# Second attention: two heads share 32 result rows, and two of four value products move into the next round

## The reference

```
q = (x @ wq).reshape(B, T, 16, 8)
lat = x @ w_down
k, v = lat @ wk_up, lat @ wv_up          # per head 8 wide
q, k = rope(q), rope(k)
scores = einsum('bqhd,bkhd->bhqk', q, k) / sqrt(8)
scores = where(page(k) <= page(q), scores, lowest)   # pages of 32 tokens
out = einsum('bhqk,bkhd->bqhd', softmax(scores), v).reshape(B, T, 128)
x = x + out @ wo
```

## Time and profile before

| what | value |
|---|---|
| median of 3 runs | 492.01 us (491.33 to 493.22) |
| the profiled execution | 490.57 us, span 488.7 us |
| mean granted TensorE clock | 0.92 of full speed |
| TensorE busy | 84% of the span, 411.0 us |
| DVE, ACT, POOL busy | 63%, 47%, 44% |

### The profile page before, as it was taken

The page is one execution under the profiler, slowest core; times in us unless marked ns, Lnnn a source line. Parts: engine busy times, 40 slices in busy tenths (PEclk is TensorE's granted clock), DMA queues, the critical chain, the costliest instruction groups (busy, mean ns, idle before and its releaser), DMA issues.

```text
span 488.7 us, 15624 instructions
## 1 busy us (share of the span) xinstructions
PE 411.0 (84%) x5250; PEld 320.9 (66%) x5251; DVE 309.4 (63%) x1125; ACT 231.5 (47%) x565; POOL 214.2 (44%) x312
## 2 busy tenths in 40 slices
PE   8898899998657899977679989989888888698980
PEld 7777588885547899854446555655555567598880
DVE  4776588888564555369557568568877655454543
ACT  2687556766304555211226756756655420255540
POOL 5443345555641444325643635643822434133440
PEclk9999999999769999988858999999999876799995
DMA  8999900000001121120000000000000000112116
GB/s 237 297 217 347 275 15 9 7 11 12 24 16 45 56 65 54 40 85 1 2 1 2 1 1 3 1 0 0 1 2 7 30 23 22 35 50 64 55 48 182
DMA packets 44339, 28.60 MB, mean 59 GB/s; under 512 B 7200, under 2 KB 40480, under 8 KB 44288
## 3 DMA queue, kind: packets, MB, share of 16 engines
q1 hardware_dynamic: 38096, 20.83, 15.4%
q0 software_dynamic: 2496, 5.13, 2.9%
q10 hardware_dynamic: 3696, 1.97, 1.4%
HBM read 12.76 MB, written 15.16 MB: 57 GB/s over the span
## 4 chain that ended last, share of the span: by engine, by line
PE 58%; DVE 17%; issue 8%; DMA 7%; ACT 5%; DVEq 2%; POOL 2%; SPq 0%; POOLq 0%; ACTq 0%
PE S L1435 7%; PE bank L1445 6%; PE S L1343 6%; PE bank L1302 6%; PE bank L1319 3%; PE bank L1475 3%; PE bank L1558 3%; DVE nm L756 3%; DMA slots<-yo,token 2%; PE bank L1329 2%; PE bank L1248 2%; PE bank L1569 2%; PE bank L1254 2%; PE S L1275 2%; DMA xg<-rows 2%
## 5 line engine op out<-in xcount | busy, mean ns | idle before, releaser
L915 ACT ACTIVATE E<-S,nmax 128x256 f32<-128x256 f32 x128 | 59.0, 477 | 39.2 <-DVE nmax L541 39.2
L1148 POOL DMA_INDIRECT slots<-yo,token x46 | 44.1, 958 | 75.5 <-DVE yo L697 74.1
L1011 ACT ACTIVATE E<-S 128x1536 f32<-128x1536 f32 x32 | 46.4, 1450 | 24.4 <-PE S L1534 24.3
L1107 POOL TENSOR_TENSOR vs<-Va,rden 128x512 f32<-128x512 f32 x32 | 33.3, 1040 | 50.5 <-DVE rden L576 48.6
L1435 PE MATMUL S<-xgT,W1s 128*128 128x128 f32 x368 | 52.9, 289 | 1.4 <-DVE xgT L683 1.3
L972 ACT ACTIVATE hT<-S,b 128x128 f32<-128x128 f32 x92 | 28.7, 363 | 44.2 <-PE S L1435 44.2
L1445 PE MATMUL bank<-W,hT 128*128 x368 | 49.2, 277 | 0.2
L1435 PEld LDWEIGHTS S<-xgT,W1s 128*128 128x128 f32 x368 | 46.2, 197 | 4.5 <-issue 2.2
L756 DVE TENSOR_REDUCE nm<-bank 128x2 f32<-128x512 f32 x64 | 41.0, 683 | 9.1 <-PE bank L1501 9.1
L1445 PEld LDWEIGHTS bank<-W,hT 128*128 128x128 f32 x368 | 45.2, 194 | 0.5 <-issue 0.5
L541 DVE TENSOR_REDUCE nmax<-S 128x4 f32<-128x1024 f32 x32 | 39.0, 1218 | 7.2 <-PE S L1343 6.8
(11 more groups left out here) (181 smaller groups left out, 954.9 us busy)
## 6 DMA issues: line engine op xcount, KB each, us to landing
rows<-zeros SPq DMA_DIRECT2D x1, 8768.0 KB, 31.5
xg<-rows SPq DMA_DIRECT2D x46, 64.5 KB
W<-in_L_ffn_W SPq DMA_DIRECT2D x1, 2048.0 KB, 10.2
x<-in_L_attn_a_x SPq DMA_DIRECT2D x4, 256.0 KB, 5.4
yg<-slots SPq DMA_DIRECT2D x8, 128.0 KB, 3.5
yg<-slots ACTq DMA_DIRECT2D x8, 128.0 KB, 3.9
slots<-yo,token POOLq DMA_INDIRECT x46
yg<-in_select SPq DMA_DIRECT2D x1, 512.0 KB, 7.8
```

The lines of the kernel that those rows point to most:

```text
L915: last = act.activation(E[:, hp, h, c, :], S[hp % 2][:, h, c * T:(c + 1) * T], ACT.Exp, bias=nmax[:, hp, k:k + 1], accum_out=den[:, hp, k: ...
L1011: act.activation(Eb[:, q % 2, :, :], S4[:, 0:3, :], ACT.Exp, scale=SCALE_B).then_inc(bs["exp"], 1)
L1107: pool.tensor_tensor(vs[:, q, :, :, :], v, r, ALU.mult).then_inc(a_vs, 1)
L1148: pool.indirect_dma_start(out=y_dram, out_offset=bass.IndirectOffsetOnAxis(token[:, turn_at, :], 0), in_=yo[:, turn_at % 2, :], in_offset=None
```

## The change

Two heads share the 32 columns: in `Vb` the heads of an even block have their values in columns 0 to 7 and a one in 8, those of an odd block in columns 16 to 23 and a one in 24. Blocks 0 and 1 (and 2 and 3) are now added into the same rows of `pb[1]`, so that a batch has two blocks of results. ACT copies two blocks out and not four; four transposes and not eight turn them back; one division does all of `att`. As the heads now lie in another order, `wo` is loaded by rows, head by head. The value products of blocks 2 and 3 both run at the start of the next round, and the fourth scores move ahead of the transposes L1623.

```diff
@@ SyncE
-            sp.dma_start(wo[:, :], wo_in).then_inc(b_loaded, 16)
...
+            for g in range(HB):
+                h = head_at(g)
+                sp.dma_start(wo[g * DB:(g + 1) * DB, :], wo_in[h * DB:(h + 1) * DB, :]).then_inc(wo_loaded, 16)
@@ the order of heads
+        def head_at(g):
+            return 8 * (g // 8) + 4 * (g % 2) + (g % 8) // 2
+        def heads(t, q):
+            return t.rearrange("p (k q j) r -> p k q j r", q=2, j=4)[:, :, q, :, :]
@@ DVE
-            def b_normal(b, u):
-                dve.wait_ge(bs["on"], b * 2 + u + 1)
-                o = pb[1][:, :].rearrange("p (h r) -> p h r", r=32)
-                dve.reciprocal(rsum[:, u, :], o[:, :, DB]).then_inc(bs["rsum"], 1)
...
+            def b_normal(b):
+                dve.wait_ge(bs["on"], b + 1)
+                o = pb[1][:, :].rearrange("p (g r) -> p g r", r=16)
+                r = rsum[:, :, :].rearrange("p u h -> p (u h)")
+                dve.reciprocal(r, o[:, :, DB]).then_inc(bs["rsum"], 1)
+                dve.wait_ge(bs["rsum"], b + 1)
                 waits(dve, bs["at"], b)
+                dve.tensor_tensor(att.rearrange("p u (h d) -> p (u h) d", d=DB), o[:, :, 0:DB],
+                                  r.unsqueeze(2).to_broadcast([P, 2 * HB, DB]), ALU.mult
...
-                if l: b_normal(b - 1, 0)
+                if l: b_normal(b - 1)
...
-                if l: b_normal(b - 1, 1)
@@ ACT
-            def b_outT(b, p, q):
-                act.wait_ge(bs["pv"], b * 4 + q + 1)
-                act.copy(OTb[:, p, q, :], pb[1][:, 0:T]).then_inc(bs["ot"], 1)
+            def b_outT(b, p, k):
+                act.wait_ge(bs["pv"], b * 4 + 2 * k + 2)
+                act.copy(OTb[:, p, k, :], pb[1][:, 0:T]).then_inc(bs["ot"], 1)
...
-                if l: b_outT(b - 1, 1 - p, 3)
+                if l: b_outT(b - 1, 1 - p, 1)
...
-                if c: b_outT(b, p, 0)
...
-                if c: b_outT(b, p, 1)
+                if c: b_outT(b, p, 0)
...
-                if c: b_outT(b, p, 2)
@@ POOL
-                z = zeros[:, :].rearrange("p (h d) -> p h d", d=DB)
-                for u in range(2):
-                    last = pool.tensor_tensor(Vb[:, p, u, :, 0:DB], vst[:, p, u, :].rearrange("p (h d) -> p h d", d=DB), z,
-                                              ALU.add)
+                z = zeros[:, :].rearrange("p (k j d) -> p k j d", j=4, d=DB)
+                for q in range(2):
+                    last = pool.tensor_tensor(heads(Vb[:, p, :, :, :].rearrange("p u h r -> p (u h) r"), q)[:, :, :, 16 * q:16 * q + DB],
+                                              heads(vst[:, p, :, :].rearrange("p u (h d) -> p (u h) d", d=DB), q), z, ALU.add)
@@ TensorE, b_values: L1558, then L1561
-                              Eb[:, q % 2, h % 2, (h // 2) * T:(h // 2 + 1) * T], start=True, stop=False)
+                              Eb[:, q % 2, h % 2, (h // 2) * T:(h // 2 + 1) * T], start=(q % 2 == 0), stop=False)
...
-                                     Eb[:, q % 2, 2, h * P:(h + 1) * P], start=False, stop=True)
+                                     Eb[:, q % 2, 2, h * P:(h + 1) * P], start=False, stop=(q % 2 == 1))
@@ TensorE, b_natural
-                for q in range(4):
-                    last = pe.transpose(pb[1][:, q * P:(q + 1) * P], OTb[:, p, q, u * P:(u + 1) * P], ident)
+                for u in range(2):
+                    for k in range(2):
+                        last = pe.transpose(pb[1][:, (2 * u + k) * P:(2 * u + k + 1) * P],
+                                            OTb[:, p, k, u * P:(u + 1) * P], ident)
@@ TensorE, b_round
                 if l:
                     waits(pe, bs["x"], b - 1)
+                    pe.wait_ge(bs["ot"], b * 2 - 1)
+                    b_values(b - 1, 1 - p, 2)
                     b_values(b - 1, 1 - p, 3)
...
-                if l: b_natural(b - 1, 1 - p, 0)
+                if l: b_natural(b - 1, 1 - p)
...
                 if c:
-                    waits(pe, bs["att"], b * 2 - 1)
+                    waits(pe, bs["att"], b)
                     b_values(b, p, 0)
                 if n: b_tk(b + 1, 1 - p, 1)
-                if l:
-                    if c: pe.wait_ge(bs["ot"], b * 4 + 1)
-                    else: pe.wait_ge(bs["att"], b * 2 - 1)
-                    b_natural(b - 1, 1 - p, 1)
...
                     b_values(b, p, 1)
+                if n: b_scores(b + 1, 1 - p, 3)
                 if l:
-                    pe.wait_ge(bs["att"], b * 2)
-                    if c: pe.wait_ge(bs["ot"], b * 4 + 2)
+                    pe.wait_ge(bs["att"], b)
+                    if c: pe.wait_ge(bs["ot"], b * 2 + 1)
                     for u in range(2):
                         last = pe.transpose(pb[1][:, u * P:(u + 1) * P], att[:, u, :], ident)
...
-                if n: b_scores(b + 1, 1 - p, 3)
                 if nnn: b_kv(b + 3)
-                if l and c: pe.wait_ge(bs["attT"], b)
-                if c:
-                    pe.wait_ge(bs["ot"], b * 4 + 2)
-                    b_values(b, p, 2)
-                    b_scoresT(b, p, 3)
-                    pe.wait_ge(bs["ot"], b * 4 + 3)
+                if c: b_scoresT(b, p, 3)
...
                 if l:
-                    if not c: pe.wait_ge(bs["attT"], b)
+                    pe.wait_ge(bs["attT"], b)
```

More of the change, by code:

```diff
@@ L181, in build @@
         OTb = vs[:, :, :, :, :].rearrange("p s h c n -> p (s h c n)").rearrange(
-            "p (a q t) -> p a q t", a=2, t=T)
+            "p (a q t) -> p a q t", a=2, t=T)[:, :, 0:2, :]
         spare = OT[:, :, :, :, :].rearrange("p h j s i -> p (h j s i)").rearrange("p (k u c) -> p k u c", k=2, u=2)
@@ L232, in build @@
         b_loaded = sem("b_loaded")
+        wo_loaded = sem("wo_loaded")
         sel_loaded = sem("sel_loaded")
@@ L1092, in _ @@
             pool.wait_ge(bs["const"], 2)
-            pool.memset(Vb[:, :, :, :, DB:DB + 1], 1.0).then_inc(bs["const"], 1)
+            for q in range(2):
+                pool.memset(heads(Vb[:, :, :, :, :].rearrange("p a u h r -> p (a u h) r"), q)[:, :, :, 16 * q + DB:16 * q + DB + 1],
+                            1.0).then_inc(bs["const"], 1)
             def a_stage(b, p):
@@ L1558, in b_values, with b_natural @@
                     pe.matmul(pb[1][32 * h:32 * h + 32, 0:T], Vb[:, p, 0, 4 * q + h, :],
-                              Eb[:, q % 2, h % 2, (h // 2) * T:(h // 2 + 1) * T], start=True, stop=False)
+                              Eb[:, q % 2, h % 2, (h // 2) * T:(h // 2 + 1) * T], start=(q % 2 == 0), stop=False)
                 for h in range(4):
                     last = pe.matmul(pb[1][32 * h:32 * h + 32, P:T], Vb[:, p, 1, 4 * q + h, :],
-                                     Eb[:, q % 2, 2, h * P:(h + 1) * P], start=False, stop=True)
+                                     Eb[:, q % 2, 2, h * P:(h + 1) * P], start=False, stop=(q % 2 == 1))
                 last.then_inc(bs["pv"], 1)
-            def b_natural(b, p, u):
-                if u == 0:
-                    pe.wait_ge(bs["ot"], b * 4 + 4)
-                for q in range(4):
-                    last = pe.transpose(pb[1][:, q * P:(q + 1) * P], OTb[:, p, q, u * P:(u + 1) * P], ident)
+            def b_natural(b, p):
+                pe.wait_ge(bs["ot"], b * 2 + 2)
+                for u in range(2):
+                    for k in range(2):
+                        last = pe.transpose(pb[1][:, (2 * u + k) * P:(2 * u + k + 1) * P],
+                                            OTb[:, p, k, u * P:(u + 1) * P], ident)
                 last.then_inc(bs["on"], 1)
@@ L1615, in b_round @@
                 if c:
-                    if l: pe.wait_ge(bs["att"], b * 2)
-                    else: pe.wait_ge(bs["ot"], b * 4 + 1)
                     b_values(b, p, 1)
+                if n: b_scores(b + 1, 1 - p, 3)
                 if l:
-                    pe.wait_ge(bs["att"], b * 2)
-                    if c: pe.wait_ge(bs["ot"], b * 4 + 2)
+                    pe.wait_ge(bs["att"], b)
+                    if c: pe.wait_ge(bs["ot"], b * 2 + 1)
                     for u in range(2):
@@ L1675, in b_router @@
                     what(router_at(b, point))
-            pe.wait_ge(b_loaded, 80)
-            pe.wait_ge(bs["const"], 3)
+            pe.wait_ge(b_loaded, 64)
+            pe.wait_ge(wo_loaded, 16 * HB)
+            pe.wait_ge(bs["const"], 4)
             pe.wait_ge(copied, len(copies))
```

3 lines of the change are left out of this document (removed).

## The result

The kernel after the change takes 500.1 us (median of four runs, 498.6 to 504.24) against 491.92 for the kernel before on the same chip (491.33 to 493.22): a ratio of 1.0151, with a 95% interval of 1.010 to 1.020. It is slower by some 8 us. I had forecast 492.4 with 495.2 as the upper end.

The account below looks back on a forecast made before the run. A fixed 6.8 us of DVE and POOL was taken to bound each round's end, not TensorE. Terms +1.5 + 0.9 - 1.3 + 0.8 - 1.4 = +0.5 us gave a median of 492.4, range 488.9 to 495.2.

Parts of the forecast that it names:

- The end of the round: TensorE ready for mask transposes 0.9 us before POOL, worth nothing; rounds 5 and 6 +0.8 us together.
- rival 3: Clock falls at the end of rounds 5 and 6: one fall costs 2.5 us, 495; two, 497; chance 0.22.
- The closing rounds: Rounds 7 and 8, with extra and leaving blocks and the second return removed: total -1.4 us, bounds -3.4 and 0.
- Deferred block: Round start, two value blocks where one stood: +0.4 us in round 3, +0.79 in round 6, +1.5 over six.
- One division for two: DVE's larger division ahead of the first maxima makes TensorE wait: +0.15 us a round, +0.9 over six.
- Second return gone: Second four return transposes go, but third scores wait for ACT's key copy: 0.22 us gained a round, -1.3 over six.
- The later L1634: End of rounds 5 and 6, attention transposes behind the fourth scores: +0.54 us in round 6, about half in round 5.
- TensorE's busy time: Sign of being right: TensorE busy 0.5 us less in each of rounds 1 to 4.
- The loads: Sixteen loads of wo for one, 586 ns each on SP's queue, behind the zero fill: priced at 0.
- The signs I had named: Right: rounds 1 to 4 at 17.1 to 17.6 us; wrong: near 16.5, or clock below 1 between 355 and 375.
- Rival 1: TensorE is the bound after all, in rounds and closing rounds: 483.6 us, or 488 for half; chance together 0.14.
- Rival 2: Closing rounds keep the upper clock: -2 us on top, 488.9 us with two stretches; chance 0.12.

Follow-up runs that it names:

- e3: Kernel after with two unread products ahead of each pair of mask transposes; 497.31 us, ratio 1.0066.
- e2: Kernel after with the one old load of wo, rows in the old order of heads; 501.42 us, ratio 1.012.
- e4: Kernel after with mask transposes and ACT's mask copy moved into the next round, behind query transposes and first value block; 493.16 us, ratio 0.999.
- e1: Kernel before with sixteen loads of wo for one; 493.45 us, ratio 0.997.
- e6: Kernel before with two unread products in round -1; five of six runs between 495.1 and 499.6 us, one 487.2, no ratio.
- e7: Kernel before with only the fourth scores moved ahead of the attention transposes L1623; 494.44 us, ratio 1.003.
- e9: Kernel before with two unread products in round 7 alone; 490.5 us, ratio 0.986.
- e5: e4 plus two unread products in round -1 and in round 7; 488.37 us, ratio 0.994 against the kernel before.
- e10: e5 with round 6's router products moved ahead of the value blocks; 490.08 us, ratio 0.985 against the kernel before.
- e11: Kernel before with mask transposes moved behind the next query transposes and the unread products of e5; 488.56 us, ratio 0.990.
- e8: Kernel after with round 6's router products moved ahead of the two value blocks; 498.41 us, ratio 1.012 against the kernel before.

## Why the prediction was wrong

**The step that failed** is "The end of the round": TensorE is ready 0.9 us before POOL, and "This is worth nothing". For the position of the mask transposes this was exact: in round 3 they follow the third scores by 7.23 us for 7.24, and the idle time in front of them is 0.7 us in rounds 2 to 4. But a wait that hides behind POOL isn't free when the clock answers to it. The 1.00 us at 272.98 and the 2.02 us at 381.82 were followed by the lower level, and e3, which fills them and moves nothing else, gives back 1.32 and 2.69 us. I had this as rival 3, with "some 2 us in one piece" (2.02 measured) and a chance of 0.22, and didn't put it into the likeliest sum because one wait of 1.26 us had stayed without a fall. Two things were off in it. I looked at rounds 5 and 6 alone and not at round 0, whose end gets the same shape. And I priced a fall at 2.5 us; they cost 1.3 and 2.7, so the size was fair on average and the number of places was not: my range ended at one fall.

**The closing rounds**, -1.4, are the second step that failed. With the clock as much at the lower level as before (0.78 in before and 0.77 in e3 from the last mask transposes to the totals, 17 to 18 us of it at 0.50), e3 needs 38.60 us and before 38.36: +0.24. Split at the router's third and fourth logits (L1254; L1267 in e3), the first value products of round 8 and the last attention transposes (L1623; L1634), it is:

```
stretch, from the end of the one above     before    e3    difference   clock before, e3
last mask transposes to third logits        10.43  10.94     +0.51        1.00  0.99
to fourth logits                             7.43   6.45     -0.98        0.54  0.50
to the value products of round 8             2.79   4.19     +1.40        1.00  0.57
to the attention transposes                  4.09   3.63     -0.46        0.98  1.00
to the totals                               13.62  13.39     -0.23        0.63  0.72
```

```profile
393.59:396.38 2.79, 2.74 (x19) 2.27 (x18) 1.86 (x12) 1.71 (x2) 0.55 (x1) 1.00 0.08 25
400.17:404.36 4.19, 4.19 (x20) 3.87 (x19) 2.46 (x15) 1.82 (x2) 1.80 (x3) 0.57 0.12 35
```

The first row is of before, the second of e3. Most edges are near their terms: +0.51 where I had 0.55 for the third router step, -0.46 where round 8 was to give 0.79 less 1.21. The block that leaves gave -0.98 where 1.44 and 0.1 of wait were to go, with a lower clock here too. What takes the rest back is where the lower level lies. In before it is over when the output product and the products behind it come; in e3 it lasts on through them, and the stretch needs 1.40 us more. The same holds in after, e2 and e4, whose stretch at 0.50 that begins near the third logits lasts 10.2 us, against 6.8 in before, e1 and e6. Whether the wait of 1.25 us in front of e3's third logits (0.20 in before) makes it longer is not tested. e7's -1.1 does not show that the early fourth scores gain by themselves: it has 3.5 us less at 0.50, which is worth more than that by the price below.

**The edges** came out near their terms, but for round 5, which cost twice its term. In us, the sum of my terms for rounds 1 to 6 against the measured differences (for round 1 that of e3, whose clock stays up there):

```
round        1      2      3      4      5      6     sum
terms      -0.04  -0.07  +0.33  -0.02  +0.41  +1.26  +1.9
measured   +0.05  +0.08  +0.48  +0.04  +0.84  +1.29  +2.8
```

- *Deferred block.* From the mask transposes to the key transposes round 3 needs 2.67 us for 2.39 (311.86 - 309.19; 308.14 - 305.75), +0.28 where I had +0.4. In round 6 the first scores come at 369.70 and 364.01, that is +0.89 after their mask transposes; I had +0.79 and the division.
- *One division for two.* L787 0.42 us as forecast, L784 0.36 for 0.26: +0.23 a round and not +0.15. That is 0.5 us of the 0.9 by which the table's sums differ.
- *Second return gone.* The third scores are released by ACT's key copy, as forecast (0.29 us of idle time, 319.82).
- *The later L1634* in rounds 5 and 6: e7 measures it alone, 0.29 and 0.55 for 0.28 and 0.54.
- *TensorE's busy time* was to fall by 0.5 us in rounds 1 to 4; it fell by 0.03 to 0.06 in rounds 2 and 4. Groups that contain a wait count as busy (the third scores take 0.53 us for four where the unhindered ones take 0.39), so the measure did not suit. What makes up the rest I did not follow.
- *The loads*, priced at 0: e1 and e2 bear it out.

In sum: rounds +2.8, closing +0.2, clock +4.0, makes 7.0 us, which is what the trace shows from the first mask transposes on. The medians differ by 8.2. The remaining 1.2 us are within what single executions differ by ahead of the second attention (2.05 us between the two profiled ones, 5.3 between before and e9, whose code there is the same); I can't say more about them. Against my sum of +0.5 the 7.7 us that are missing are 4.0 of clock, 0.9 of edges, 1.6 of closing rounds and these 1.2.

**The signs I had named.** Those of being right came for the lengths of rounds 2 and 4, the release of the third scores, the division and round 6, and the wait in front of the mask transposes with 0.7 us for 0.8 to 1; they failed for rounds 1 and 3 and for the closing rounds. Neither sign of being wrong came: the clock stood at 1.00 from 355 to 375 and fell outside the stretch that I had named.

**The other rivals.** Rival 1 (TensorE is the bound): rounds 2 and 4 did not shorten, and e7's filled waits moved nothing, so no. Rival 2 (closing rounds keep the upper clock): the opposite came, though the upper level is worth what it supposed: e9, with 1.1 us of unread products, holds it to about 402 us, 21 us behind its last mask transposes where before held it for 11, and closes in 1.4 us less.

## What to carry to other kernels

Ahead of a wait that another engine ends, work taken off TensorE shortened nothing here and lengthened what followed, as the clock fell behind the longer wait: look at the granted clock of the stretch behind every wait that a change makes longer, in every round that has it and not in the one that was studied, and in more than one trace. What helped was to have TensorE do something there, by moving the waiting instruction behind work that is ready (e4, e5) or by a few products that nobody reads (e3, e9); neither kept the clock up each time (e5 near 275 us, e10 from 380). And before a change is credited with a gain, the same repair belongs on the kernel without it: e11 showed that the change had brought nothing of e5's gain in the rounds at full clock.

## What the hardware showed that I had not expected

- Waits of 1.00 us were followed by the lower level in after and e2 (e2: 1.00 us in front of 274.38, granted 0.53 from 274 to 276). In e8 1.01 us at the same place (272.75) were not, and its round 1 lasts 17.54 us. At the end of round 5, 2.02 us of wait left the clock at 1.00 in after and e2 and were followed by 0.50 in e8. At the end of round 6 the same 2.02 us were followed by a fall in all three. Before, e1, e6, e7 and e9, with waits of at most 0.59 us at these places, have no fall at any of them. The same instructions with the same waits fall in one execution and not in the next, so one trace shows that a fall is possible and not how often it comes.
- A microsecond at the lower level cost some 0.4 us; at half the rate it can cost at most 0.5. After spends 24 us of its last 42.78 at 0.50 (0.28 x 42.78 / 0.5) and e3 17.6 of 40.10, so 6.4 us at 0.50 cost 2.7. e10 and e5, with the same closing code, have 30.9 and 5.6 us at 0.50 and need 44.16 and 35.07: 9.1 us for 25.3. Round 1 paid 1.3 for 3.4.
- Behind two unread products, 1.1 us of TensorE's time, the full clock lasted some 10 us longer in the closing rounds of e9 (21 us from the last mask transposes for 11 in before). In e10 the same products stood in a stretch at 0.50 that lasted on to 404.
- A reciprocal of 128 x 32 out of PSUM takes 0.36 us where 128 x 16 takes 0.26. It grows by 0.10 at twice the size, almost as much as the multiplication behind it (0.42 for 0.29), where I had allowed 0.03.
